# One decoder layer on one core: a load moved forward in the queue, a late wait, sums in halves, key rows by ScalarE, one activation moved

## The chip, the core and the metric

The kernel runs on one core of one Trainium2 chip. Its engines are TensorE (PE; PEld is its loading of weights), VectorE (DVE), ScalarE (ACT), GpSimd (POOL) and SyncE (SP, which here only issues DMAs); each has a queue of its own and they meet by semaphores. The metric is the device time of one execution in microseconds (us).

## The reference, cut to what matters

```
x = x + mamba(layernorm(x))                 # x: 8 batches x 224 rows x 512
x = x + cross_attention(layernorm(x), ctx)  # 16 heads of 32; ctx: 8 x 750 x 256
x = x + moe(layernorm(x))                   # 4 experts, the 2 likeliest for each row

mamba:  h[d, n] = h[d, n] * exp(A[d, n] * dt[d]) + dt[d] * x[d] * B[n]   # 224 steps in order
        y[d] = sum over the 16 n of h[d, n] * C[n];  y = (y + x * D) * silu(z);  return y @ W_out
attention: softmax((q Wq + bq)(k Wk + bk)^T / sqrt(32)) (v Wv + bv), then @ Wo + bo
moe:    p = softmax(gelu(x @ rW1 + rb1) @ rW2 + rb2)
        for each of its 2 experts: out += p * (gelu(x @ We1 + be1) @ We2 + be2)
```

## The kernel before, in words

Four stages follow one another, each in a block of its own; a block ends when all its engines and the DMAs that it awaits are done. They are the input products of the Mamba part, the state space (`state_space`, about 335 to 1017 us of the span), the attention with the router (`attention`, 1017 to 1826 us) and the experts (`experts`, from 1826 us).

**State space.** The work is 64 units (8 batches x 8 blocks of 128 channels), each in 4 segments of 56 time steps. For each segment TensorE fills PSUM, VectorE runs the scan (L917) and GpSimd multiplies the states by C (L804, counted by `hc_done`); the 16 states are then added up by TensorE, as products of the identity with `hc` into `yps`. For all units but the last this is `sums` (L955): for each state one product over all 224 columns, its four segments at once. The last unit's is `last_sums` (L959 to L968): it goes segment by segment, awaits each by `hc_done`, and has 4 x 16 products of 56 columns. Each float32 product shows as two records in the trace. `outputs` (DVE, L899 and L904) then makes `y`, and SP stores it (L705).

**Attention.** Every engine walks the same list `steps()` (iteration `it` from -1 to 9, slot `sl` from 0 to 15), and its order is written out by hand. With a = it + 1, c = it - 1 and last = it - 2, iteration `it` does the scores and softmax of batch `it` (one head a slot), the first half of batch a (Mamba's output product `project` L1699, the residual `residual1` L1305, the norm L1322 to L1339, `turn_norm` L1712, the queries L1726), the output and hidden layer of batch c, and the routing of batch `last`. In a slot, TensorE makes scores for two halves of the rows (L1633), VectorE takes their negated maxima (L1299, into `nmax`), ScalarE turns two such rows into the queries (L1549), TensorE makes the turned scores (L1659) with the key rows, ScalarE exponentiates (L1543), GpSimd adds up key tiles (`row_sum`, L1255 to L1261), and TensorE multiplies by the values (`values`, L1672) and by ones (`row_sums`, L1683).

`k3` holds the keys in its first 96 partitions; the two more rows (96 and 97) hold 1 and 0 in turn, by head parity, for all of its eight head places. They are written once: GpSimd sets them to zero (L1224) and adds a one-hot column (L1227 to L1229), which SP loads (L1178). Then GpSimd sets constants, waits for the residual of batch 0 and adds the output bias to it (`with_bias`, L1271, slot 13 of iteration -1). ScalarE first waits for three small loads (`w_loaded`) and scales Wq and bq (L1586).

SP's queue in iteration -1: `load_g(1)` at slot 5; stores of the first queries and `load_first_queries` at slot 8 (12 loads, L1164); `load_values` at slot 10 (4 loads of 375 KB, L1142); seven weights and constants at slot 11 (Wo, rb1, rW1, rW2, rb2, two small ones: L1219); `load_x(1)` at slot 14 (L1129, 448 KB: batch 1's rows of x into `xt`, after waits for `x1b_done` and `xn_done`). In iteration 0 follow `load_g(2)` at slot 5 (L1124, 896 KB) and `load_keys(2)` at slot 6 (L1135, three loads of 375 KB). `residual1(1, 0)`, in DVE's queue at slot 2 of iteration 0 between the two maxima, awaits `x_loaded`.

`gelu(last)` (ScalarE, L1572) stands in slot 0, behind that slot's exponentials and ahead of `turned_max`. In iteration 8 (`it == B`) only three heads' exponentials are left, in slots 0 to 2. The product of the gelu, `logit_parts` (L1762), stands in slot 4 of TensorE's queue, behind the values of slot 3.

**Experts.** Tiles of 256 rows go through 16 hidden blocks. VectorE makes the low parts of the hidden values (`results`, L2080) and at the end of a tile adds the second bias `b2` (L2086). `first` of expert 0 makes low parts of weights (L2055), the gates (L2059 to L2061) and then waits for `b2_loaded`, ahead of all tiles; SP issues that load at L1944.

## Time and profile before

| | |
|---|---|
| three runs | 2675.36, 2679.37, 2680.34 us; median 2679.37 |
| the profiled execution, its own time | 2675.31 us |
| its span | 2673.5 us |
| PE / PEld / DVE / ACT / POOL busy | 2404.6 / 1976.3 / 1452.0 / 1219.3 / 1373.0 us |
| mean granted TensorE clock | 0.948 of full |

All times in rows are us from the start of the span unless marked ns. A timeline row gives start, duration, engine, line, operation and operands; a time in square brackets is the idle time of that engine before it and what ended it. A row with xN merges N instructions that follow one another, from the first's start to the last's end. SPq is SP's queue issuing DMAs. A granted clock of 1.00 is TensorE's 2.4 GHz, 0.50 is 1.2 GHz.

### The profile page before, as it was taken

Reading aid. Unit: us, or ns where it says so; the run is one execution under the profiler, and the core shown is the slowest. Engines: PE = TensorE matmul, PEld = TensorE weight load, DVE = VectorE, ACT = ScalarE, POOL = GpSimd, SP = SyncE. Lnnn points to the kernel's source line nnn. Section 1 sums busy time; section 2 is a strip of 40 time slices with the busy share of each in tenths; the row PEclk is TensorE's granted clock in tenths of the full one; section 3 lists DMA queues with packets and bytes.
Section 4 is the critical chain, followed back from the end, with each engine's and each line's share of the span. In section 5 each row is a group of like instructions: output and inputs, shape, how many; then the busy total and the mean of one; then the engine's idle time right before and its main releaser. Section 6 shows DMA issues by size and latency. Waiting matters only on the chain. (4 is left out here: it accounts for less than half of the span.)

```text
span 2673.5 us, 39214 instructions
## 1 busy us (share of the span) xinstructions
PE 2404.6 (90%) x14240; PEld 1976.3 (74%) x14240; DVE 1452.0 (54%) x2034; ACT 1219.3 (46%) x2645; POOL 1373.0 (51%) x947
## 2 busy tenths in 40 slices
PE   7999499999999997589999999884989989998994
PEld 6867388888888885457766667564878878888883
DVE  7714599999999982355766666644121121121222
ACT  4345377777777651334544444433323333333331
POOL 2323477777777773365556656635460450019712
PEclk9999699999999998689999999886989999999997
DMA  4326956666666563455554655605230130003413
GB/s 121 125 69 220 268 177 208 195 188 174 200 199 207 165 188 101 129 116 122 136 135 115 143 120 124 156 21 170 79 112 22 63 118 16 16 31 95 116 34 118
DMA packets 235990, 341.72 MB, mean 128 GB/s; under 512 B 34706, under 2 KB 164306, under 8 KB 234690
## 3 DMA queue, kind: packets, MB, share of 16 engines
q1 hardware_dynamic: 213250, 279.89, 37.6%
q0 software_dynamic: 13728, 47.19, 5.7%
q10 hardware_dynamic: 8864, 12.72, 1.4%
q8 instruction: 86, 1.41, 0.2%
q14 instruction: 62, 0.51, 0.1%
HBM read 212.08 MB, written 127.65 MB: 127 GB/s over the span
## 5 line engine op out<-in xcount | busy, mean ns | idle before, releaser
L917 DVE TENSOR_TENSOR_SCAN s_h<-s_decay,s_ub 128x928 f32<-128x928 f32 x256 | 527.3, 2080 | 13.9 <-PE s_ub L944 7.1
L955 PE MATMUL s_yps<-s_hc,identity 128*128 128x224 f32 x2016 | 423.1, 353 | 0.0
L2080 DVE TENSOR_TENSOR e_hl<-e_ps,e_hh 128x256 fp32r<-128x256 f32 x256 | 108.6, 425 | 571.6 <-ACT e_ps L2130 571.2
L847 ACT ACTIVATE s_decay<-s_dt,s_A 128x224 f32<-128x224 f32 x1024 | 387.9, 470 | 20.8 <-DVE s_h L917 18.8
L955 PEld LDWEIGHTS s_yps<-s_hc,identity 128*128 128x128 f32 x2016 | 362.5, 190 | 0.8 <-issue 0.5
L1299 DVE TENSOR_REDUCE t_nmax<-t_ps 112x1 fp32r<-112x752 f32 x256 | 240.3, 938 | 218.8 <-PE t_ps L1633 218.0
L1255 POOL TENSOR_TENSOR t_part<-t_pT 125x672 f32<-125x672 f32 x128 | 206.9, 1616 | 275.1 <-ACT t_pT L1543 271.7
L2129 ACT ACTIVATE e_hh<-e_ps,e_b 128x256 fp32r<-128x256 f32 x256 | 122.0, 477 | 432.7 <-PE e_ps L2156 432.4
L2154 PE MATMUL e_ps<-e_xTh,e_w1h 128*128 128x256 f32 x1024 | 292.9, 286 | 23.3 <-DVE e_xTl L2072 23.3
L1543 ACT ACTIVATE t_pT<-t_ps 125x448 f32<-125x448 f32 x384 | 181.2, 546 | 273.7 <-PE t_ps L1659 266.9
L804 POOL TENSOR_TENSOR s_hc<-s_h,s_Cc 128x896 f32<-128x896 f32 x128 | 247.5, 1939 | 90.2 <-DVE s_h L917 47.4
L804 POOL TENSOR_TENSOR s_hc<-s_h,carry 128x896 f32<-128x896 f32 x128 | 247.6, 1940 | 88.9 <-DVE s_h L917 47.6
L2155 PE MATMUL e_ps<-e_xTl,e_w1h 128*128 128x256 f32 x1024 | 291.8, 285 | 0.0
L2156 PE MATMUL e_ps<-e_xTh,e_w1l 128*128 128x256 f32 x1024 | 290.9, 284 | 0.0
L1980 POOL TENSOR_TENSOR e_w1h<-carry,e_one 128x2048 fp32r<-128x2048 f32 x13 | 46.9, 3608 | 376.4 <-PE e_ps L2156 376.2
L1633 PE MATMUL t_ps<-t_k,t_q 96*112 96x376 f32 x512 | 187.7, 449 | 49.1 <-DVE t_nmax L1299 44.8
L2154 PE MATMUL e_ps<-e_w2h,e_hh 128*128 128x512 f32 x512 | 206.0, 402 | 22.1 <-DVE e_hl L2080 22.1
L2154 PEld LDWEIGHTS e_ps<-e_xTh,e_w1h 128*128 128x128 f32 x1024 | 197.6, 193 | 34.4 <-issue 24.6
L2155 PEld LDWEIGHTS e_ps<-e_xTl,e_w1h 128*128 128x128 f32 x1024 | 197.3, 193 | 9.3
L2156 PE MATMUL e_ps<-e_w2h,e_hl 128*128 128x512 f32 x512 | 202.7, 396 | 0.0
L2155 PE MATMUL e_ps<-e_w2l,e_hh 128*128 128x512 f32 x512 | 202.2, 395 | 0.0
L2156 PEld LDWEIGHTS e_ps<-e_xTh,e_w1l 128*128 128x128 f32 x1024 | 198.7, 194 | 0.0
(231 smaller groups left out, 4607.3 us busy)
## 6 DMA issues: line engine op xcount, KB each, us to landing
s_ut<-ut_d SPq DMA_DIRECT2D x192, 128.0 KB, 3.3
carry<-in_L_ffn_We POOLq DMA_DIRECT2D x24, 1024.0 KB, 5.7
t_k<-kh_d SPq DMA_DIRECT2D x64, 375.0 KB, 6.3
xs_d<-s_zero SPq DMA_DIRECT2D x30, 512.0 KB, 3.6
ut_d<-a_x SPq DMA_DIRECT2D x32, 448.0 KB, 5.4
kh_d<-s_kh SPq DMA_DIRECT2D x32, 375.0 KB, 2.8
kl_d<-s_kl SPq DMA_DIRECT2D x32, 375.0 KB, 3.1
v_d<-s_v SPq DMA_DIRECT2D x48, 250.0 KB
```

Of the source, the lines that this page charges most:

```text
L804: nc.gpsimd.tensor_tensor(hc[:, u % 2, k], h[:, u % 2, k, :, 2:SLOT], Cc[b % 2][:, k], ALU.mult).then_inc(hc_done, 1)
L847: ins = nc.scalar.activation(decay[:, u % 2, :, n, 2:SLOT], dts[:, u % 2].rearrange("p (s t) -> p s t", s=NSEG), ACT.Exp, scale=A[:, u % C ...
L917: nc.vector.tensor_tensor_scan(h[:, u % 2, k].rearrange("p n t -> p (n t)"), decay[:, u % 2, k].rearrange("p n t -> p (n t)"), ub[:, s % 2 ...
L955: ins = nc.tensor.matmul(yps[:, u % 2, 0:L], ident[:], hc[:, u % 2, :, n], start=(n == 0), stop=(n == NS - 1))
L1255: nc.gpsimd.tensor_tensor(part[:], p[:, 0:3], p[:, 3:6], ALU.add).then_inc(sum_step, 1)
L1299: nc.vector.tensor_reduce(nmax[:, u, h:h + 1], ps[0:TT, 0:2, 0:EVEN], AX.XY, ALU.max, negate=True).then_inc(max_done, 1)
L1543: nc.scalar.activation(pT[:, g % PT, 2 * i:2 * i + 2], ps[0:CT, TURN_BANK + i, 0:2 * L].rearrange("p (i t) -> p i t", i=2), ACT.Exp).then_ ...
L1633: ins = nc.tensor.matmul(ps[0:TT, i, 0:EVEN], q3[0:ROWS3, b % 2, h, u * TT:(u + 1) * TT], k3[0:ROWS3, J % 2, h % 4, i * (CTX - EVEN):i * ( ...
L2129: nc.scalar.activation(hh[:, c % RING], hidden_in, ACT.Gelu, bias=bias).then_inc(S["h_high"], 1)
L2154: nc.tensor.matmul(out, sh, mh, start=first, stop=False)
L2155: nc.tensor.matmul(out, sh, ml, start=False, stop=False)
L2156: return nc.tensor.matmul(out, sl, mh, start=False, stop=last)
```

## The change

The edits of the diff:

- `last_sums` goes by halves: it waits for segments 0 and 1, makes 16 products of 112 columns, waits for segments 2 and 3 and makes 16 more.
- The two extra key rows are written by ScalarE in four activations (scale 0 and a bias column of the identity), ahead of its wait for the small loads. GpSimd's memset and four additions, the one-hot tile and its load go, and so does its first semaphore.
- `load_x(1)` moves from slot 14 to slot 9 of iteration -1 in SP's queue; the later batches' loads stay at slot 14.
- In iteration 8 the gelu moves from slot 0 to slot 4.
- The wait for `b2_loaded` moves from behind the gates to the bias addition at each tile's end.
- The wait for `y_done` in `last_sums` stands ahead of the first wait for `hc_done`.

```
--- before.py
+++ after.py
@@ -958,13 +958,12 @@
 
             def last_sums(u):
 
-                for k in range(NSEG):
-                    pe.wait_ge(hc_done, NSEG * u + k + 1)
-                    if k == 0:
-                        pe.wait_ge(y_done, u - 1)
+                pe.wait_ge(y_done, u - 1)
+                for half in range(2):
+                    pe.wait_ge(hc_done, NSEG * u + 2 * half + 2)
                     for n in range(NS):
-                        ins = nc.tensor.matmul(yps[:, u % 2, k * SEG:(k + 1) * SEG], ident[:], hc[:, u % 2, k, n],
-                                               start=(n == 0), stop=(n == NS - 1))
+                        ins = nc.tensor.matmul(yps[:, u % 2, half * L // 2:(half + 1) * L // 2], ident[:],
+                                               hc[:, u % 2, 2 * half:2 * half + 2, n], start=(n == 0), stop=(n == NS - 1))
                 ins.then_inc(sum_done, 1)
 
             def keys_values(u, pieces):
@@ -1045,7 +1044,6 @@
         wo, rw1, rw2 = sb("wo", [P, KC, DM]), sb("rw1", [P, KC, RH]), sb("rw2", [P, RC, DK])
         bqc, bvc, rb1c = sb("bqc", [P, KC]), sb("bvc", [P, KC]), sb("rb1c", [P, RC])
         bor, rb2r = sb("bor", [P, DM]), sb("rb2r", [P, E])
-        onehot = sb("onehot", [ROWS3 + 2, 2])
         ones = sb("ones", [CT, DK])
         xb = sb("xb", [TT, 2, 2, DM])
         k3 = sb("k3", [ROWS3 + 2, 2, 4, CTX], F32R)
@@ -1082,7 +1080,7 @@
         x2_stored = sem("x2_stored")
         route, shifted, exped, masked, ranked, rank_read, indexed, counted = (
             sem(n) for n in ("route", "shifted", "exped", "masked", "ranked", "rank_read", "indexed", "counted"))
-        consts_set, rows_zeroed, rows_set, q_scaled = (sem(n) for n in ("consts_set", "rows_zeroed", "rows_set", "q_scaled"))
+        consts_set, rows_set, q_scaled = (sem(n) for n in ("consts_set", "rows_set", "q_scaled"))
         score_mm, max_done, turn_mm, turn_done = (sem(n) for n in ("score_mm", "max_done", "turn_mm", "turn_done"))
         st_mm, exp_done, sum_step, sum_done = (sem(n) for n in ("st_mm", "exp_done", "sum_step", "sum_done"))
         pv_mm, sums_mm, rinv_done, o_read, o_done = (sem(n) for n in ("pv_mm", "sums_mm", "rinv_done", "o_read", "o_done"))
@@ -1092,7 +1090,7 @@
         q_mm, q_high, q_low = sem("q_mm"), sem("q_high"), sem("q_low")
         rh_mm, rh_pre, rh_done, lp_mm, lp_done, lg_mm, lg_done = (
             sem(n) for n in ("rh_mm", "rh_pre", "rh_done", "lp_mm", "lp_done", "lg_mm", "lg_done"))
-        N_W, N_REST, N_SET = 3, 7, 22
+        N_W, N_REST, N_SET = 2, 7, 22
         ROUTE = 18
         FAR = float(E * SLOTS)
 
@@ -1175,7 +1173,6 @@
                     We1[0].rearrange("(k p) n -> p k n", p=P)[:, :, g * DM:(g + 1) * DM]
                 sp.dma_start(carry[:, n * KC * DM:(n + 1) * KC * DM].rearrange("p (k n) -> p k n", n=DM), src).then_inc(w_first[n], 16)
 
-            sp.dma_start(onehot[ROWS3:ROWS3 + 2], ident_in[0:2, 0:2]).then_inc(w_loaded, 16)
             for dst, src in ((bqc[:], bq), (bvc[:], bv)):
                 sp.dma_start(dst, src).then_inc(w_loaded, 16)
             load_keys(0)
@@ -1205,10 +1202,12 @@
                     sp.dma_start(x2_d[c], xb[:, c % 2]).then_inc(x2_stored, 16)
                 if it == -1 and sl == 5:
                     load_g(1)
+                if it == -1 and sl == 9:
+                    load_x(1)
                 if it == -1 and sl == 10:
                     for j in range(KC):
                         load_values(j)
-                if sl == 14 and among(a + 1, B):
+                if sl == 14 and it >= 0 and among(a + 1, B):
                     load_x(a + 1)
                 if it == B - 1 and 1 <= sl <= 4:
                     load_first_weights(sl - 1)
@@ -1221,13 +1220,6 @@
 
         @block.gpsimd
         def _(pool):
-            nc.gpsimd.memset(k3[ROWS3:ROWS3 + 2].bitcast(F32), 0.0).then_inc(rows_zeroed, 1)
-            pool.wait_ge(rows_zeroed, 1)
-            pool.wait_ge(w_loaded, 16 * N_W)
-            for r in range(4):
-                nc.gpsimd.tensor_scalar(k3[ROWS3:ROWS3 + 2, :, r], k3[ROWS3:ROWS3 + 2, :, r].bitcast(F32),
-                                        onehot[ROWS3:ROWS3 + 2, r % 2:r % 2 + 1], None, ALU.add).then_inc(rows_set, 1)
-            pool.wait_ge(rows_set, 4)
             nc.gpsimd.memset(ones[:], 1.0).then_inc(consts_set, 1)
 
             for t in state_sems:
@@ -1581,6 +1573,11 @@
                 act.wait_ge(shifted, b + 1)
                 nc.scalar.activation(p[:], p[:], ACT.Exp).then_inc(exped, 1)
 
+
+            two = slice(ROWS3, ROWS3 + 2)
+            for r in range(4):
+                nc.scalar.activation(k3[two, :, r], ident[two, 0:2].unsqueeze(2).to_broadcast([2, 2, CTX]), ACT.Identity, scale=0.0,
+                                     bias=ident[two, ROWS3 + r % 2:ROWS3 + r % 2 + 1]).then_inc(rows_set, 1)
             act.wait_ge(w_loaded, 16 * N_W)
             for t in (wq, bqc[:]):
                 nc.scalar.activation(t, t, ACT.Copy, scale=float(DK) ** -0.5).then_inc(q_scaled, 1)
@@ -1596,7 +1593,7 @@
                     high_queries(a, 2 * sl - 16)
                 if among(s - LAG, STEPS):
                     exponentials(s - LAG)
-                if sl == 0 and among(last, B):
+                if sl == (4 if it == B else 0) and among(last, B):
                     gelu(last)
                 if sl == 7 and among(a, B):
                     turned_norm(a, 0, 0)
@@ -2082,6 +2079,7 @@
                     wait(dve, "l2_mm", n * HC + HC)
 
                     wait(dve, "y_stored", n * 16)
+                    wait(dve, "b2_loaded", 16)
                     for s in range(HALVES):
                         v.tensor_tensor(y[:, s], ps[:, Y_BANK + s], b2[:, e], ALU.add).then_inc(S["y_done"], 1)
 
@@ -2091,7 +2089,6 @@
                         for n in range(2, 4):
                             low_weights(n)
                         gates()
-                        wait(dve, "b2_loaded", 16)
 
                 expert_tiles(dve, e, first, results)
```

## Rows read from the trace of the kernel before
**Rows 1.** Windows: us; busy (count) of PE, PEld, DVE, ACT, POOL; clock; DMA.
```profile
1000.00:1017.20 17.20, 14.04 (x126) 13.90 (x125) 1.61 (x4) 0.00 (x0) 0.78 (x1) 1.00 0.07 25
...
1066.00:1090.30 24.30, 2.00 (x8) 0.66 (x6) 1.60 (x3) 1.81 (x2) 0.00 (x0) 0.62 0.66 194
```
**Rows 2.** Timeline, end of the state space: start us, us, engine, line.
```profile
998.85 1.93 POOL L804 TENSOR_TENSOR s_hc<-s_h,s_Cc 128x896 f32<-128x896 f32 x1 [1.12 <-DVE s_h L917]
...
996.61 3.19 PE L955 MATMUL s_yps<-s_hc,identity 128*128 128x224 f32 x16
999.64 14.39 PE L966 MATMUL s_yps<-s_hc,identity 128*128 128x56 f32 x128
```
**Rows 3.** Timeline, the attention's first 25 us.
```profile
1019.64 1.91 ACT L1586 ACTIVATE carry<-carry 128x2048 f32<-128x2048 f32 x1 [22.23 <-DMA t_bvc<-in_L_xattn_bv]
...
1022.44 16.57 POOL L1228 TENSOR_SCALAR t_k<-t_k,t_onehot 2x1500 fp32r<-2x1500 f32 x4
...
1032.97 0.69 DVE L1305 TENSOR_TENSOR carry<-t_ps,carry 112x512 f32<-112x512 f32 x1 [5.44 <-PE t_ps L1699]
...
1034.64 0.23 DVE L1322 TENSOR_SCALAR t_rstd<-t_mv 112x2 f32<-112x2 f32 x1
...
1036.68 3.05 DVE L1339 TENSOR_SCALAR t_xn<-carry,t_mv,t_rstd 112x512 f32<-112x512 f32 x2
```
**Rows 4.** Timeline near 1146 us, then line L1339 over the span (ns min/median/max).
```profile
1146.00 2.49 POOL L1271 TENSOR_TENSOR t_xb<-carry,t_bor 112x512 f32<-112x512 f32 x2
...
1146.34 2.29 DVE L1456 TENSOR_SCALAR t_oT<-t_rinv,t_bvc 128x224 f32<-128x224 f32 x1
...
L1339 DVE TENSOR_SCALAR t_xn<-carry,t_mv,t_rstd x16: 529/547/2604, 1036.7 to 1627.2; 112x512 f32<-112x512 f32 x16
```
**Rows 5.** Timeline, 1058 to 1093 us.
```profile
1058.96 10.86 SPq L1142 DMA_DIRECT2D t_v<-v_d  x4
...
1061.84 1.88 PE L1699 MATMUL t_ps<-carry 128*112 128x512 f32 x4
...
1064.11 0.94 DVE L1299 TENSOR_REDUCE t_nmax<-t_ps 112x1 fp32r<-112x752 f32 x1 [1.12 <-PE t_ps L1633]
...
1083.62 0.33 SPq L1129 DMA_DIRECT2D carry<-in_x  x1
1088.70 0.69 DVE L1305 TENSOR_TENSOR carry<-t_ps,carry 112x512 f32<-112x512 f32 x1 [23.65 <-DMA carry<-in_x]
...
1092.29 3.62 PE L1699 MATMUL t_ps<-carry 128*112 128x512 f32 x4
```
**Rows 6.** Line L1129, the seven later loads of x rows: time to landing.
```profile
DMA to landing us min/median/max: 5.1/7.3/8.3
```
**Rows 7.** Line L1135, the 96 key loads, to landing; timeline, first scores of keys 2.
```profile
DMA to landing us min/median/max: 3.7/5.6/10.5
...
1118.19 0.60 PE L1633 MATMUL t_ps<-t_k,t_q 96*112 96x376 f32 x2
```
**Rows 8.** Timeline, end of the attention's last batch.
```profile
1759.23 1.70 ACT L1572 ACTIVATE t_rh<-t_rh 128x1792 f32<-128x1792 f32 x1
...
1762.40 1.28 ACT L1543 ACT_TABLE_LOAD   x1 [0.92 <-PE t_ps L1659]
...
1765.19 1.61 POOL L1255 TENSOR_TENSOR t_part<-t_pT 125x672 f32<-125x672 f32 x1 [3.02 <-ACT t_pT L1543]
1766.75 4.71 PE L1672 MATMUL t_ps<-t_pT,t_v 125*32 125x224 f32 x48 [0.79 <-issue]
...
1772.53 0.59 PE L1683 MATMUL t_ps<-t_rsum,t_ones 125*32 125x224 f32 x8
```
**Rows 9.** The second-layer bias: issue, landing of line L1944, DVE behind its wait.
```profile
1841.33 0.51 SPq L1944 DMA_DIRECT2D e_b<-in_L_ffn_be  x1
...
DMA to landing us min/median/max: 9.0/9.0/9.0
...
1852.01 1.09 DVE L2080 TENSOR_TENSOR e_hl<-e_ps,e_hh 128x256 fp32r<-128x256 f32 x3 [0.41 <-DVE e_gate L2061]
```

More of the change, by code:

```diff
@@ L959, in last_sums @@
             def last_sums(u):
-                for k in range(NSEG):
-                    pe.wait_ge(hc_done, NSEG * u + k + 1)
-                    if k == 0:
-                        pe.wait_ge(y_done, u - 1)
+                pe.wait_ge(y_done, u - 1)
+                for half in range(2):
+                    pe.wait_ge(hc_done, NSEG * u + 2 * half + 2)
                     for n in range(NS):
-                        ins = nc.tensor.matmul(yps[:, u % 2, k * SEG:(k + 1) * SEG], ident[:], hc[:, u % 2, k, n],
-                                               start=(n == 0), stop=(n == NS - 1))
+                        ins = nc.tensor.matmul(yps[:, u % 2, half * L // 2:(half + 1) * L // 2], ident[:],
+                                               hc[:, u % 2, 2 * half:2 * half + 2, n], start=(n == 0), stop=(n == NS - 1))
                 ins.then_inc(sum_done, 1)
@@ L1047, in attention @@
         bor, rb2r = sb("bor", [P, DM]), sb("rb2r", [P, E])
-        onehot = sb("onehot", [ROWS3 + 2, 2])
         ones = sb("ones", [CT, DK])
@@ L1084, in attention @@
             sem(n) for n in ("route", "shifted", "exped", "masked", "ranked", "rank_read", "indexed", "counted"))
-        consts_set, rows_zeroed, rows_set, q_scaled = (sem(n) for n in ("consts_set", "rows_zeroed", "rows_set", "q_scaled"))
+        consts_set, rows_set, q_scaled = (sem(n) for n in ("consts_set", "rows_set", "q_scaled"))
         score_mm, max_done, turn_mm, turn_done = (sem(n) for n in ("score_mm", "max_done", "turn_mm", "turn_done"))
@@ L1094, in attention @@
             sem(n) for n in ("rh_mm", "rh_pre", "rh_done", "lp_mm", "lp_done", "lg_mm", "lg_done"))
-        N_W, N_REST, N_SET = 3, 7, 22
+        N_W, N_REST, N_SET = 2, 7, 22
         ROUTE = 18
@@ L1207, in _ @@
                     load_g(1)
+                if it == -1 and sl == 9:
+                    load_x(1)
                 if it == -1 and sl == 10:
@@ L1210, in _ @@
                         load_values(j)
-                if sl == 14 and among(a + 1, B):
+                if sl == 14 and it >= 0 and among(a + 1, B):
                     load_x(a + 1)
@@ L1223, in _ @@
         def _(pool):
-            nc.gpsimd.memset(k3[ROWS3:ROWS3 + 2].bitcast(F32), 0.0).then_inc(rows_zeroed, 1)
-            pool.wait_ge(rows_zeroed, 1)
-            pool.wait_ge(w_loaded, 16 * N_W)
-            for r in range(4):
-                nc.gpsimd.tensor_scalar(k3[ROWS3:ROWS3 + 2, :, r], k3[ROWS3:ROWS3 + 2, :, r].bitcast(F32),
-                                        onehot[ROWS3:ROWS3 + 2, r % 2:r % 2 + 1], None, ALU.add).then_inc(rows_set, 1)
-            pool.wait_ge(rows_set, 4)
             nc.gpsimd.memset(ones[:], 1.0).then_inc(consts_set, 1)
@@ L1582, in probabilities @@
                 nc.scalar.activation(p[:], p[:], ACT.Exp).then_inc(exped, 1)
+            two = slice(ROWS3, ROWS3 + 2)
+            for r in range(4):
+                nc.scalar.activation(k3[two, :, r], ident[two, 0:2].unsqueeze(2).to_broadcast([2, 2, CTX]), ACT.Identity, scale=0.0,
+                                     bias=ident[two, ROWS3 + r % 2:ROWS3 + r % 2 + 1]).then_inc(rows_set, 1)
             act.wait_ge(w_loaded, 16 * N_W)
@@ L1598, in _ @@
                     exponentials(s - LAG)
-                if sl == 0 and among(last, B):
+                if sl == (4 if it == B else 0) and among(last, B):
                     gelu(last)
@@ L2084, in results @@
                     wait(dve, "y_stored", n * 16)
+                    wait(dve, "b2_loaded", 16)
                     for s in range(HALVES):
@@ L2093, in first @@
                         gates()
-                        wait(dve, "b2_loaded", 16)
                 expert_tiles(dve, e, first, results)
```

1 line of the change is left out of this document (removed).

## The prediction

> **What bounds the kernel now.** I first read the page's busy shares: TensorE is busy most of the span, so a gain has to come from stretches in which it idles, works slowly or does work that can shrink. The windows show two. From 1000 to 1017.2 us TensorE works alone, at the full clock, and nobody else has work [rows 1]. From 1066 to 1090.3 us all four engines stand still together [rows 1]. The timeline says what ends each. The first is `last_sums`: 128 records of 56 columns, 14.39 us, begun when the last segment's product with C was already running (998.85 to 1000.78), so that from the second segment on it waits for nobody [rows 2]. The second is DVE's residual of batch 1, which sat 23.65 us for a DMA that SP issued only at 1083.62 us, behind the values and the weights; DVE holds the next maximum behind it, and everybody waits for that maximum [rows 5]. The same reading of the attention's first 25 us and of its end gives two short stalls on the chain [rows 3, 8].
>
> **The parts.** Sums are made against the profiled execution's own 2675.31 us.
>
> *Sums in halves.* 64 float32 products become 32, so 128 records become 64. A record costs 14.39 / 128 = 0.112 us at 56 columns and 3.19 / 16 = 0.199 us at 224 [rows 2]. At 112 columns the price lies between. If the 0.112 us is the loading of the 128 columns of weights, the same for both, then 64 x 0.112 = 7.2 us, a gain of 7.2; at the price of 224 columns it is 12.8 us, a gain of 1.6. Streaming twice 56 columns more cannot cost less than before, so 7.2 is the best. I take it: scaled down from 224 columns, the streaming of 112 takes 0.10 us, less than 0.112. Of the two waits the second is over at 1000.78, while the first half runs until 1003.2, so they cost nothing. Here a rule speaks against the change. The Trainium skill, page "TensorE: Matmul & The Clock Gate", section "Measured speedup vs the span model", says that a weight load overlaps a product in flight only when they use different row groups; here both use all rows. By that rule and the page's load price (columns / 1.2 ns, 107 ns) a record would be load plus streaming, 154 ns at 56 columns and 200 ns at 112, and the gain at measured start would be 14.4 - 12.8 = 1.6 us, for a sum of 30.1. The 0.112 us that the trace has at 56 columns is well under that 154, so trace and rule disagree. From the last sum to the block's end all follows in a row (DVE's two operations, the store), so the gain is whole.
>
> *Key rows by ScalarE.* Off GpSimd go 16.57 us and a memset. On ScalarE come four activations of 1500 elements a partition; from 1.91 us for 2048 [rows 3] each takes 1.40 us, 5.6 in all, from 1017.2 to 1022.8. Wq is then scaled by 1024.8 instead of 1021.5; even at the 4.1 us that GpSimd took for each it would be 1035.5, ahead of the end of the normalisation at 1039.7, which the first query needs too. Hidden, at no cost. The gain is elsewhere: DVE's normalisation took 3.05 us for two [rows 3] instead of 2 x 0.55 [rows 4], its first one ending just after GpSimd's last of the four at 1039.01; DVE waited for GpSimd. Gone alone, this gives 2.05 us. But what is next on GpSimd? It now reaches `with_bias` early, and runs its 2.49 us from 1033.7, when DVE's second residual of batch 0 (L1305) is done [rows 3], to 1036.2. In its middle, at 1034.64, DVE has the small operation L1322 [rows 3]. In rows 4 just such a DVE operation, begun beside GpSimd's pair, lasted 2.29 us, to the end of both. So L1322 ends at 1036.3, 1.4 us later than before, and of 2.05 us some 0.6 stay. The Trainium skill, page "SBUF — State Buffer", has the shared ports held for one whole instruction by whoever began first; by that rule L1322 would get them between GpSimd's two, at 1035.0, and the gain would be some 1.9 us, the sum 37.0. The row speaks for the pair as a whole. I take 0.6, between 0.6 and 2.05. The dropped one-hot load frees SP 0.3 us long before it matters.
>
> *Rows of batch 1.* Issued behind the first queries, at 1058.96 where the first value load now stands [rows 5]. Both waits in `load_x` are over by then. This load took 5.1 us to land (1083.62 to 1088.7), later batches' up to 8.3 [rows 6], so x is there between 1064.1 and 1067.3. DVE wants it after the maximum of 1064.11, at 1065.05 [rows 5]. So 23.65 us go, and 0 to 2.2 come back; I take 0, for only small loads stand ahead. What is moved past are four value loads and seven weight loads: they get later by the wire time of 448 KB, a microsecond or two. The values are wanted some 25 us after, the weights in iteration 1. What is late next: SP gets through the weights only by about 1084.5, as before, since these are held by the queue and not by engines. Then come the 896 KB of `load_g(2)` and the three key loads, the last issued near 1086. These land 3.7 to 10.5 us later [rows 7], at 1089.7 to 1096.5; TensorE wants them at 1118.19 - 23.65 = 1094.54 [rows 7]. That gives 0 to 2.0 us; with g in front I take 0.5. The stall also left TensorE cold: four records of `project` took 3.62 us behind it and 1.88 before it [rows 5], where the granted clock had been 1.2 and 2.4 GHz. This gives back 1.7 us in the first slot; as low stretches may come elsewhere, the bounds are -1.7 and +3.5. Together 23.65 - 0.5 + 1.7 = 24.9 us, between 17.7 and 27.2.
>
> *The gelu.* In iteration 8 it took ScalarE with a table load 3.0 us ahead of the turned maximum, and another table load of 1.28 us before the exponentials [rows 8]: 4.3 us off their chain. But the chain ends at GpSimd, whose sums release the product with ones at 1772.53; GpSimd had only 3.02 us of idle time before the last but one of them [rows 8], its scatter being just ahead. So 3.0 us. Behind the exponentials the gelu and its load (3.0 us) run beside the values, 4.71 us on TensorE [rows 8]; without that cover the 3.0 would come back. I take 3.0, between 0 and 3.0.
>
> *The bias.* Issued at 1841.33, landed 9.0 us later at 1850.3; DVE worked on the gates until 1851.6 and began the low parts at 1852.01 after 0.41 us [rows 9]. The wait was hidden by the gates: no gain beyond 0.4. It now stands in front of the bias additions of all 16 tiles, with the load long there. Queued behind it are only these and, for the store, ACT's DMA; on the chain stand the four tiles that end an expert, at most 4 x 0.41 = 1.6 us. I take 0.
>
> Sum: 7.2 + 0.6 + 24.9 + 3.0 = 35.7 us, so 2639.6 for this execution. The median of three runs is 4.06 us above it; carried over, 2643.7 us.
>
> **The rivals.** *A, the forecast*, all four gains within their bounds (31 to 40 us): 0.72.
> *B, the DMA queue gives part of it back.* x, the values, g(2) or keys(2) land so late that a new DMA wait of 5 to 12 us stands in slots 2 to 8. For: in 1066 to 1090 the queue was never empty, 0.66 busy [rows 1], and nothing makes these bytes fewer. Against: the key loads' slowest landing leaves 2 us. Price 8: 2651.7. Chance 0.12.
> *C, a record costs load and streaming*, as the skill's rule has it or as the row at 224 columns would: the gain on the sums is 1.6 instead of 7.2, 2649.3. The 56-column row speaks against it. 0.09.
> *D, the change does not do what it says*: x is not what DVE waited for, or its new place still waits, because `x1b_done` comes late. Then 10.8 us stay: 2668.6. Against: issue plus landing, 1083.62 + 5.1, is just the 1088.70 at which DVE went on. 0.05.
> *E, slower.* The keys of group 2, in slot 8 of iteration 0, behind x, values, weights and g: each microsecond beyond 1094.5 is one on the chain. It decides from 1094.5 + 35.7 = 1130 us, 44 us after the issue; the slowest of 96 took 10.5 [rows 7]. At 50 us it would give 2685. 0.02 with all else that could make it not faster.
>
> **The numbers.** A, C and most of B are inside 2634 to 2655: the low end is the best of each part (39.9 us) against the fastest run, 2635.5, a little widened; the high end is 25 us of gain against the median. What a measurement of this kernel can tell from no change is about 0.2%, 5.4 us. Faster by more: A to D, 0.98. Within it 0.01, slower 0.01.
>
> **What would show it.** `last_sums` as 64 records in about 7.2 us; DVE's L1322 lasting 1.6 us and its two normalisations 1.1; x issued before the values and no wait of 20 us at L1305; any key wait at the first scores of group 2 under 2 us; GpSimd without idle time before its last two sums and the product of the gelu right behind the values; no change around L2080. I am wrong if the sums take over 9 us, if a DMA wait over 5 us stands between slots 2 and 9, or if the stage from 1118 us on is not the same length as before.

## The result and the profile after

| us | before | after |
|---|---|---|
| median (range, runs) | 2679.86 (2675.36 to 2681.37, 4) | 2647.03 (2643.26 to 2648.53, 4) |
| the profiled execution, its own time | 2675.31 | 2648.53 |
| its span | 2673.5 | 2646.7 |
| PE / DVE / ACT / POOL busy | 2404.6 / 1452.0 / 1219.3 / 1373.0 | 2391.3 / 1459.1 / 1224.4 / 1351.7 |
| mean granted TensorE clock | 0.948 | 0.955 |

The ratio is 0.9878, 95% interval [0.9861, 0.9895]: 32.8 us less by the medians, 26.8 by the two profiled executions. The two differ because the profiled execution of before is as fast as the fastest of its four (2675.36), and that of after is the slowest of its own; the rows below come from these two. The forecast was 2643.7, within 2634 to 2655. So the total is right within 3.3 us. The parts are less so. I cut both timelines at the same instructions (first product of the attention's block, first transpose, first maximum of slots 0, 3, 7 and 8 and of batch 1, last maximum, last product with ones, first product of the experts); each number is a difference of start times in the trace.

| stretch, us | before | after | difference |
|---|---|---|---|
| up to the attention's block | 1017.3 | 1012.1 | -5.2 |
| block to first transpose | 22.06 | 20.27 | -1.8 |
| to the first maximum | 14.85 | 13.75 | -1.1 |
| to slot 3 | 37.11 | 12.53 | -24.6 |
| slots 3 to 7 | 20.25 | 16.23 | -4.0 |
| slot 7 to slot 8 | 7.28 | 13.13 | **+5.85** |
| to batch 1 | 42.87 | 42.06 | -0.8 |
| batch 1 to the last maximum | 591.91 | 599.71 | **+7.8** |
| to the last product with ones | 18.92 | 15.96 | -3.0 |
| to the experts' first product | 62.93 | 63.45 | +0.5 |
| to the end | 838.04 | 837.49 | -0.55 |

They add up to the span's 26.8 us. Three rows are positive: +5.85, which I had sized at 0.5, +7.8, which I had not seen at all, and +0.5 at the end of the attention, which the gelu gives back. The -1.1 between the first transpose and the first maximum I didn't forecast, and no run isolates it.

The start of the changed stretch, from the timeline of after (start, duration, engine, line, operation); it answers to [rows 2, 3]:
```profile
1001.58 7.29 PE L965 MATMUL s_yps<-s_hc,identity 128*128 128x112 f32 x64
...
1012.10 5.83 ACT L1579 ACTIVATE t_k<-identity 2x1500 fp32r<-2x1500 f32 x4 [12.75 <-PEq L597]
...
1028.66 2.51 POOL L1263 TENSOR_TENSOR t_xb<-carry,t_bor 112x512 f32<-112x512 f32 x2 [11.49 <-DVE carry L1297]
...
1029.49 0.49 DVE L1314 TENSOR_SCALAR t_rstd<-t_mv 112x2 f32<-112x2 f32 x1
...
1031.79 1.00 DVE L1331 TENSOR_SCALAR t_xn<-carry,t_mv,t_rstd 112x512 f32<-112x512 f32 x2
```
The last sums are 64 records in 7.29 us, 0.114 each, where 128 took 14.39: 7.1 less. They began 1.9 us later in the span than before, after 1000 us of unchanged code; in the kernels below that share the new sums the block's start lies anywhere from 1008.2 to 1014.1, so those 1.9 us are not the change's. The small operation L1314 lasted 0.49 us, not the 1.6 that I forecast, and ended at 1029.98, just behind the end of GpSimd's first addition (1029.95).

Rows and keys in iteration 0, same timeline, against [rows 5, 7]:
```profile
1049.94 0.37 SPq L1127 DMA_DIRECT2D carry<-in_x  x1
1050.35 11.36 SPq L1140 DMA_DIRECT2D t_v<-v_d  x4
...
1055.24 0.68 DVE L1297 TENSOR_TENSOR carry<-t_ps,carry 112x512 f32<-112x512 f32 x1
...
1074.40 2.05 SPq L1133 DMA_DIRECT2D t_k<-kh_d  x1
1076.49 1.13 SPq L1133 DMA_DIRECT2D t_k<-kl_d  x1
1077.67 0.46 SPq L1133 DMA_DIRECT2D t_k<-kh_d  x1
...
1078.55 3.38 PE L1669 MATMUL t_ps<-t_pT,t_v 125*32 125x224 f32 x48
...
1087.15 0.84 PE L1630 MATMUL t_ps<-t_k,t_q 96*112 96x376 f32 x2 [5.22 <-issue]
...
1088.03 0.94 DVE L1291 TENSOR_REDUCE t_nmax<-t_ps 112x1 fp32r<-112x752 f32 x1 [9.51 <-PE t_ps L1630]
```
The residual has no wait left. But before the first scores of key group 2 TensorE sat 5.22 us, though nothing on the engines was late. "Issue" here means only that the profile found no releaser. The windows around it (us; busy and count of PE, PEld, DVE, ACT, POOL; clock; DMA share and GB/s), first those that answer to [rows 1]:
```profile
1000.00:1012.10 12.10, 8.88 (x74) 8.71 (x73) 2.41 (x5) 0.00 (x0) 1.94 (x2) 1.00 0.20 59
1066.00:1070.00 4.00, 2.58 (x15) 1.82 (x14) 2.97 (x4) 2.70 (x4) 3.07 (x4) 1.00 1.01 327
1070.00:1074.00 4.00, 2.67 (x12) 1.65 (x11) 3.52 (x9) 2.92 (x6) 1.55 (x3) 0.52 1.03 408
1074.00:1078.00 4.00, 3.90 (x16) 3.18 (x17) 1.66 (x3) 2.47 (x5) 3.66 (x4) 0.50 1.08 295
1078.00:1082.00 4.00, 3.93 (x52) 2.00 (x50) 0.52 (x1) 0.54 (x1) 2.30 (x3) 0.70 1.10 176
1082.00:1087.00 5.00, 0.00 (x0) 0.00 (x0) 0.00 (x0) 0.00 (x0) 0.00 (x0) 1.00 0.68 161
```
From 1082 to 1087 all engines stood still together while the DMA engines, full since 1066, were at 0.68. It is the picture of [rows 1] again, five microseconds instead of twenty.

The end of the attention, against [rows 8]:
```profile
1738.29 1.28 ACT L1564 ACT_TABLE_LOAD   x1
1738.37 4.54 PE L1669 MATMUL t_ps<-t_pT,t_v 125*32 125x224 f32 x48 [0.79 <-issue]
1738.40 1.62 POOL L1247 TENSOR_TENSOR t_part<-t_pT 125x672 f32<-125x672 f32 x1
...
1742.73 0.95 PE L1759 MATMUL t_ps<-t_rh,t_rw 128*32 128x224 f32 x16
...
1745.76 0.77 PE L1680 MATMUL t_ps<-t_rsum,t_ones 125*32 125x224 f32 x8 [2.09 <-POOL t_rsum L1253]
...
1749.01 9.02 PE L1736 MATMUL t_ps<-t_wo,t_oT 128*112 128x512 f32 x16 [1.64 <-DVE t_oT L1448]
```
GpSimd's 3.02 us of idle time is gone, and the gelu runs beside the values. It now ends at 1741.29, so its product has it in time.

Where the +7.8 us came from shows in slot 13 of batch 1 in this timeline:
```profile
1200.54 2.55 POOL L1263 TENSOR_TENSOR t_xb<-carry,t_bor 112x512 f32<-112x512 f32 x2 [1.05 <-issue]
...
1201.08 3.70 DVE L1448 TENSOR_SCALAR t_oT<-t_rinv,t_bvc 128x224 f32<-128x224 f32 x1
...
1203.04 1.60 POOL L1247 TENSOR_TENSOR t_part<-t_pT 125x672 f32<-125x672 f32 x1
```
A DVE operation of 0.34 us, begun beside GpSimd's bias additions, lasted 3.70 us: to the end of both and of GpSimd's next one as well. The next maximum stands behind it.

### The profile page after: what moved, and what is told of

The parts are those of the page before. It is cut to its first block and busy times, and to the rows that moved or that the text cites. A ratio compares the mean times of both kernels' runs of the same rounds, so it can differ in the third digit from the quotient of the medians.

```text
span 2646.7 us, 39098 instructions
## 1 busy us (share of the span) xinstructions
PE 2391.3 (90%) x14176; PEld 1967.2 (74%) x14176; DVE 1459.1 (55%) x2034; ACT 1224.4 (46%) x2649; POOL 1351.7 (51%) x942
## 5 line engine op out<-in xcount | busy, mean ns | idle before, releaser
L2077 DVE TENSOR_TENSOR e_hl<-e_ps,e_hh 128x256 fp32r<-128x256 f32 x256 | 108.5, 425 | 571.1 <-ACT e_ps L2127 570.7
```

## The experiments

The change is a bundle, so first its parts. All ratios are against the kernel before, run beside it.

| kernel | median (range, runs), us | ratio, 95% |
|---|---|---|
| e1_x_late | 2667.16 (2652.61 to 2675.94, 10) | 0.9964 [0.9944, 0.9984] |
| e2_weights_late | 2652.28 (2640.38 to 2660.03, 5) | 0.9916 [0.9884, 0.9948] |
| e3_x_only | 2656.31 (2653.10 to 2662.84, 4) | 0.9930 [0.9903, 0.9957] |
| e5_bias_later | 2639.00 (2636.18 to 2642.24, 4) | 0.9860 [0.9838, 0.9882] |
| f1_rows_gpsimd | 2640.66 (2639.54 to 2644.29, 4) | 0.9876 [0.9860, 0.9893] |
| f2_gelu_early | 2642.40 (2638.30 to 2643.54, 4) | 0.9877 [0.9860, 0.9893] |
| f3_b2_early | 2636.65 (2631.19 to 2640.72, 4) | 0.9855 [0.9837, 0.9874] |
| f4_rw1_late | 2630.25 (2626.98 to 2634.25, 4) | 0.9830 [0.9813, 0.9846] |
| g0_changed_again | 2644.72 (2640.05 to 2656.99, 6) | 0.9889 [0.9869, 0.9908] |
| e6_bias_later_before | 2668.21 (2663.05 to 2672.64, 10) | 0.9973 [0.9959, 0.9988] |
| f5_sums_whole | 2637.91 (2633.09 to 2641.84, 4) | 0.9876 [0.9855, 0.9896] |
| g1_best | 2631.35 (2625.60 to 2634.67, 4) | 0.9840 [0.9817, 0.9863] |

The kernel before had medians of 2674.45, 2674.89 and 2675.35 us beside them (first four rows, next four, last four). Medians of different groups of four rows are best compared by their ratios.

**The rows of x: one undone, one alone.** e1 is the changed kernel with the load back in slot 14:
```
-                if it == -1 and sl == 9:
-                    load_x(1)
-                if sl == 14 and it >= 0 and among(a + 1, B):
+                if sl == 14 and among(a + 1, B):
                     load_x(a + 1)
```


> The changed kernel with batch 1's rows of x back at slot 14 of iteration -1, behind values and weights. Theory (the stall was the place of this load in SP's queue; the forecast's 23.65 us, 0.9 more by the fourth slot, 4.0 from TensorE's full clock until slot 7, less a wait of 5.2 us for the keys of group 2): a DMA stall of 22 to 25 us returns at the residual of batch 1, the key wait is gone, first maximum to first of batch 1 is 105 to 109 us instead of 84.0, the time is 22 to 25 us above the changed kernel's. Rival (other edits of the change took most of the stall away, such as GpSimd reaching its bias addition early): the stall is under 10 us and the time within 10 us of the changed kernel's.

The stall came back. Timeline of e1, DVE's residual of batch 1:
```profile
1077.39 0.69 DVE L1295 TENSOR_TENSOR carry<-t_ps,carry 112x512 f32<-112x512 f32 x1 [21.94 <-DMA carry<-in_x]
```
By the same cuts as above e1 has 33.72 us to slot 3 (+21.2), 19.68 for slots 3 to 7 (+3.45) and 7.53 from slot 7 to 8 (-5.6). So the wait for keys is the price of having removed the wait for x, and the slots behind the stall had been slow with it, not only the first: the granted clock over slots 3 to 7 is 0.67 before, 0.76 in e1 and 0.85 in the changed kernel. From the first maximum of slot 0 to that of batch 1 e1 takes 103.8 us, just under the 105 to 109 expected. From the first maximum to slot 8 that is 60.93 us against 41.89 of the changed kernel, a net 19.0; the medians of e1 and g0 lie 22.4 apart, their ratios 0.0075 or 20.1.

e3 is the kernel before with only this move:
```
+                if it == -1 and sl == 9:
+                    load_x(1)
-                if sl == 14 and among(a + 1, B):
+                if sl == 14 and it >= 0 and among(a + 1, B):
```


> The kernel before with only the load of batch 1's x moved to slot 9. Theory (the move alone is worth its stall, plus clock, less the key wait): 20 to 25 us less than before, first maximum to first of batch 1 at 84 to 86 us. If the move needs GpSimd freed of the key rows: its bias addition of batch 0 ends at 1046.7, before SP reaches slot 9 at 1058.9, so no difference is expected; the rival says SP waits for it and less than 15 us are gained.

18.1 us by the medians, with 14.68 us from slot 7 to 8, and 64.64 - 45.10 = 19.5 from the first maximum to slot 8. The changed kernel's own trace has 64.64 - 41.89 = 22.75 there. The part is worth 18 to 23 us, below my 24.9 and for e3 below the 20 to 25 expected of it (87.1 us to batch 1 instead of 84 to 86); rival B would have left 16.9. The truth lay between the two.

**What holds the keys up.** e2 moves all seven weight loads of slot 11 from iteration -1 to iteration 0:
```
-                if it == -1 and sl == 11:
+                if it == 0 and sl == 11:
                     sp.wait_ge(consts_set, 2)
```


> The changed kernel with the seven weight and constant loads of iteration -1 (3 MB) moved behind the queries of iteration 0 in SP's queue (slot 11). Theory (the 5.2 us in which TensorE waits before slot 8 are the key loads of group 2 queued behind g(2), weights and values): these keys land 5 us or more before they are wanted, the wait is gone, slot 7 to slot 8 takes 7 to 8 us instead of 13.1, and the time is 4 to 6 us lower if no later DMA takes its place. Rival (the wait is the values' or the engines' own order, not the queue): slot 7 to slot 8 stays at 12 to 13.5 us, no time gained. A third way: the weights now delay x, values or keys in slots 12 to 15, and the gain is given back there.

Slot 7 to 8 fell from 13.13 to 7.78 us, so the weights in front were indeed what delayed the keys. They did it in two ways. In the changed kernel the last of the three keys was issued 31.5 us after the first maximum of slot 0, in e2 25.6 us after it; and from issue to landing the three took, in the changed kernel, in e2 and in f4 (below), in this order:
```profile
DMA to landing us min/median/max: 8.7/9.1/9.4
...
DMA to landing us min/median/max: 4.2/5.7/7.0
...
DMA to landing us min/median/max: 6.7/8.1/11.5
```
So the last key was there 40.9 us after that maximum in the changed kernel and 32.6 in e2, and TensorE was ready for it at 35.8 and 35.9. But batch 0's remainder grew from 42.06 to 47.17. Timeline of e2, first scores of batch 1, whose keys were issued from 1114.64 us on:
```profile
1127.68 0.94 PE L1630 MATMUL t_ps<-t_k,t_q 96*112 96x376 f32 x2 [5.26 <-DMA t_k<-kh_d]
```
Here the profile names the releaser: the key load. The weights now stood in front of the next group of keys, and the wait went there nearly whole (5.35 us off, 5.1 on); the median is no lower than the changed kernel's. f4 moves only the largest, rW1 (2 MB), and puts it right behind the keys of group 2 (on top of e5, below):
```
-                    for dst, src in ((wo[:], rows(Wo)), (rb1c[:], rb1), (rw1[:], rows(rW1)), (rw2[:, :, 0:E], rows(rW2)),
+                    for dst, src in ((wo[:], rows(Wo)), (rb1c[:], rb1), (rw2[:, :, 0:E], rows(rW2)),
...
+                if it == 0 and sl == 7:
+                    sp.dma_start(rw1[:], rows(rW1)).then_inc(rest_loaded, 16)
```


> The changed kernel with the later bias addition, and with one weight load (rW1, 2 MB of the 3) moved behind the key loads of group 2 in SP's queue (slot 7 of iteration 0). Theory (these keys wait for 3 MB of weights in the queue; moving all of them to slot 11 only carried the wait to the next batch's first slot): slot 7 to slot 8 takes 7.5 to 9 us instead of 12 to 13, and slot 8 to the first of batch 1 stays at 42 to 43 us: 3 to 5 us faster. Rival (any place gives it back: values and queries' stores of slots 8 and 9 stand behind it now): slot 8 to batch 1 grows by what slot 7 gains.

Timeline of f4, keys, rW1 and the first scores of group 2:
```profile
1069.23 0.32 SPq L1133 DMA_DIRECT2D t_k<-kh_d  x1
1069.60 0.43 SPq L1133 DMA_DIRECT2D t_k<-kl_d  x1
1070.07 0.43 SPq L1133 DMA_DIRECT2D t_k<-kh_d  x1
1070.55 0.43 SPq L1196 DMA_DIRECT2D t_rw<-in_L_ffn_rW  x1
...
1081.69 0.57 PE L1632 MATMUL t_ps<-t_k,t_q 96*112 96x376 f32 x2 [1.10 <-issue]
```
TensorE waits 1.10 us instead of 5.22; slot 7 to 8 takes 9.00 us, and nothing took its place: the rest of batch 0 is 42.24 and the middle batches 590.65. The last key's landing did not get shorter (11.5 us); it was issued 6.0 us earlier. The median is the lowest of its four rows, 6.4 us under f3's and 10.4 under f1's, the two others of the four that keep the gelu late; their intervals touch at 0.9837 to 0.9846 for f3 and are apart for f1.

**The middle batches.** e5 is the changed kernel with GpSimd's bias additions one slot later, except for batch 0; e6 has the same edit on the kernel before:
```
-                if sl == 13 and among(it + 1, B):
+                if sl == (13 if it == -1 else 14) and among(it + 1, B):
                     with_bias(it + 1)
```


> The changed kernel with GpSimd's addition of the output bias one slot later (14 instead of 13) for all batches but the first. Theory (in slot 13 of the later batches this 2.5 us pair runs into DVE's scaling of the attention's output, which waits until GpSimd is through, and how often it does is a matter of phase: the seven slot-13 gaps of the changed kernel sum to 44.5 us against 34.5 before): all slot-13 gaps at 4.3 to 4.6 us, first of batch 1 to the last maximum at 585 to 590 us instead of 599.7, the time 8 to 13 us below the changed kernel's. Rival (the longer gaps are a DMA's or the clock's): gaps of 6 to 9 us stay in several batches and the time stays within 3 us.

Line L1448 over the whole span, shortest, median and longest in ns, first in the changed kernel:
```profile
L1448 DVE TENSOR_SCALAR t_oT<-t_rinv,t_bvc x32: 335/337/3696, 1099.7 to 1748.6; 128x224 f32<-128x224 f32 x32
```
then in e5:
```profile
L1448 DVE TENSOR_SCALAR t_oT<-t_rinv,t_bvc x32: 335/336/1619, 1101.4 to 1739.2; 128x224 f32<-128x224 f32 x32
```
In e5 the same two operations no longer meet in slot 13; its timeline has the DVE one first:
```profile
1203.16 0.34 DVE L1448 TENSOR_SCALAR t_oT<-t_rinv,t_bvc 128x224 f32<-128x224 f32 x1
...
1206.71 2.54 POOL L1263 TENSOR_TENSOR t_xb<-carry,t_bor 112x512 f32<-112x512 f32 x2
```
The time from the first maximum of slot 13 to that of slot 14, batches 1 to 7, is 7.5, 6.6, 9.2, 6.1, 4.6, 6.1, 4.4 us in the changed kernel and 4.4 in all seven in e5, 13.8 us less; the stretch from batch 1 to the last maximum goes from 599.71 to 588.39. So the collisions carry the +7.8: slot 13 alone is 10.1 us longer than before. Was that the change's doing?

> The kernel before with GpSimd's bias addition of all batches but the first one slot later. Theory (the same collisions cost the kernel before 4 us in its profiled execution and more in its slower ones): all slot-13 gaps at 4.3 to 4.7 us, 3 to 8 us less than before. Rival (only the changed kernel's phase meets them): within 2 us of before.

> The changed kernel once more, unaltered, on the chip of this call. Theory (slot 13 of the later batches is a matter of phase from execution to execution): the seven slot-13 gaps sum to another value than the 44.5 us of its first trace, somewhere between 33 and 48, while block start to the first transpose (20.3), the fourth slot (12.5 from the first maximum) and slot 7 to 8 (12 to 13.5) repeat within 1 us; the time is 26 to 35 us below the kernel before. Rival (the gaps belong to the changed kernel's order): the same batches have the same gaps within 0.5 us.

In the kernel before the gaps of slot 13 were 4.4 but for one of 8.0, and 590.63 us in e6 stand beside 591.91: 1.3 us in the trace, though the median fell by 7.1 (interval 0.9959 to 0.9988). g0, the changed kernel once more, has 608.57 us there with gaps of up to 9.3. So both kernels can collide. Whether GpSimd and DVE meet is a matter of how the engines stand to each other: before, GpSimd's pair began at 1233.53, after DVE's operation at 1232.72, in the slot in which they overlapped after. The two traces of the changed kernel have collisions in most batches and the one of before in one; whether the change makes them more frequent, or one trace of before was a lucky one, these runs don't settle. The unprofiled executions speak for luck: g0's profiled one is the slowest of its six, and by the medians moving the additions takes 7.1 us off the kernel before, and off the changed kernel 4.8 (ratio 0.9878 to 0.9860) to 7.8 (0.9889 to 0.9860), which is no more.

What a meeting costs depends on when it begins. All fourteen traces together have 37 in which DVE's operation (L1314, L1448 and their likes in the other kernels) began while GpSimd was in the first of its two bias additions, of 1.3 us each. DVE's operation ended 0.02 to 0.18 us behind the end of the second in the 14 begun 0 to 0.48 us after GpSimd's first, behind a third instruction in the 5 begun 0.51 to 0.60 us after it, behind the first alone in the 17 begun 0.64 to 0.99 us after it, and behind the third in one begun at 1.22. So a shift of a tenth of a microsecond can cost three. Why it falls out so, no run shows. The trace of before, too, has one that ended behind the first addition, in slot 13 of batch 5:
```profile
1488.05 2.54 POOL L1271 TENSOR_TENSOR t_xb<-carry,t_bor 112x512 f32<-112x512 f32 x2 [1.27 <-issue]
...
1488.77 0.68 DVE L1456 TENSOR_SCALAR t_oT<-t_rinv,t_bvc 128x224 f32<-128x224 f32 x1
```

**The small parts**, each undone on top of e5, so that the collisions don't blur them. f1, key rows by GpSimd again (its memset, four additions, the one-hot tile and load):
```
+            for r in range(4):
+                nc.gpsimd.tensor_scalar(k3[ROWS3:ROWS3 + 2, :, r], k3[ROWS3:ROWS3 + 2, :, r].bitcast(F32),
+                                        onehot[ROWS3:ROWS3 + 2, r % 2:r % 2 + 1], None, ALU.add).then_inc(rows_set, 1)
...
-            for r in range(4):
-                nc.scalar.activation(k3[two, :, r], ident[two, 0:2].unsqueeze(2).to_broadcast([2, 2, CTX]), ACT.Identity, scale=0.0,
-                                     bias=ident[two, ROWS3 + r % 2:ROWS3 + r % 2 + 1]).then_inc(rows_set, 1)
```


> The changed kernel with the later bias addition (GpSimd's slot 14), and with the two extra key rows written by GpSimd again, with the one-hot load. Theory (DVE's normalisation waits for GpSimd's running instruction, and with the rows gone DVE's small operation L1314 is let in between GpSimd's two bias additions): block start to the first transpose back from 20.3 to 22.1 us or up to 24.2 (it depends on where in GpSimd's 4.07 us instruction DVE comes), DVE's two normalisations back at 3 us or more, the rest as before: 2 to 4 us slower than with the rows on ScalarE. Rival (the forecast's 0.6 us, the gain comes from elsewhere, such as ScalarE's start): the stretch stays within 0.7 us of 20.3.

Timeline of f1, the block's start:
```profile
1013.38 16.57 POOL L1229 TENSOR_SCALAR t_k<-t_k,t_onehot 2x1500 fp32r<-2x1500 f32 x4
1025.58 0.23 DVE L1323 TENSOR_SCALAR t_rstd<-t_mv 112x2 f32<-112x2 f32 x1
...
1027.63 3.05 DVE L1340 TENSOR_SCALAR t_xn<-carry,t_mv,t_rstd 112x512 f32<-112x512 f32 x2
```
These are the durations of [rows 3] again, and the first transpose comes 22.07 us into the block. In the ten kernels with rows by ScalarE it comes after 19.90 to 21.64. Most of that spread lies ahead of the second residual, in TensorE's 15 products: 15.7 us from the block's start at a granted clock of 0.89, 16.7 to 17.1 us at 0.82 to 0.84 in f2, f5 and g0. From the second residual to the first transpose it takes 6.4 us in before, e6 and f1 and 4.6 in nine of the ten, so the part is worth 1.8 us; the medians (2640.66 against 2639.00 of e5 and 2636.65 of f3) can't resolve it. With the rows on GpSimd it can also be worse: in e3 DVE's small operation began at 1034.03, 0.13 us after one of GpSimd's four, and lasted 3.97 us; the first transpose came after 24.18 us.

g1 takes that further (f4, the sums of f5, and GpSimd's first bias additions held until DVE's normalisation is done):
```
                 if b == 0:
                     pool.wait_ge(bo_loaded, 16)
+                    pool.wait_ge(xn_done[0], 2)
```


> Put together: the changed kernel with the later bias addition, rW1 behind the key loads of group 2, sums as a whole, and the first batch's bias addition held until its two normalisations are done. Theory: slot 13 at 4.4 us, slot 7 to 8 at 9 us, block start to the first transpose at 19.9 to 20.1 us (DVE's L1314 at 0.17 to 0.23 us instead of 0.49), 9 to 13 us less than the changed kernel of this call. Rival: GpSimd's held addition makes the load of batch 1's x late (then a stall at its residual), or the key wait is taken over by another DMA.

Timeline of g1:
```profile
1028.03 0.17 DVE L1315 TENSOR_SCALAR t_rstd<-t_mv 112x2 f32<-112x2 f32 x1
...
1031.15 2.51 POOL L1264 TENSOR_TENSOR t_xb<-carry,t_bor 112x512 f32<-112x512 f32 x2 [15.40 <-DVE t_xn L1332]
```
Alone, L1315 takes 0.17 us. So beside GpSimd it had lost 0.3 us (0.49), and 4.25 us from the second residual to the first transpose against 4.57 is that 0.3. As a whole g1 is no faster than f4.

f2, the gelu in slot 0 again in iteration 8:
```
-                if sl == (4 if it == B else 0) and among(last, B):
+                if sl == 0 and among(last, B):
```


> The changed kernel with the later bias addition, and with the gelu of iteration 8 back in slot 0. Theory (GpSimd's sums are the chain's end there, and had 3.0 us of idle time to lose): last maximum to the last product with ones 18.9 us instead of 15.9, 3 us slower. Rival (it is the product of the gelu behind the values that counts): within 1 us.

Timeline of f2, end of the attention's last batch:
```profile
1731.41 1.61 POOL L1247 TENSOR_TENSOR t_part<-t_pT 125x672 f32<-125x672 f32 x1 [3.01 <-ACT t_pT L1535]
...
1741.83 8.61 PE L1736 MATMUL t_ps<-t_wo,t_oT 128*112 128x512 f32 x16 [2.00 <-DVE t_oT L1448]
```
GpSimd's idle 3.01 us is back, and 18.92 us from the last maximum to the product with ones. The next stretch tells something else: up to the experts it takes 62.75 us here and 64.92 in f3. The 16 output products L1736 took 8.61 us in f2, 9.02 in the changed kernel and 10.02 in f3. Windows of exactly these products, in f2:
```profile
1741.80:1750.50 8.70, 8.61 (x16) 3.32 (x16) 1.14 (x5) 1.49 (x2) 0.00 (x0) 0.82 0.06 21
```
and in f3:
```profile
1737.30:1747.40 10.10, 10.02 (x16) 3.73 (x16) 1.15 (x5) 1.49 (x2) 0.00 (x0) 0.71 0.05 18
```
The granted clock was 0.82 of full in the one and 0.71 in the other. Both stretches together are 81.67 to 81.85 us in the four traces with the gelu early and 79.20 to 80.98 in the ten with it late. So of the 3.0 us between 0.7 and 2.7 stay. The medians (2642.40 against 2639.00 of e5 and 2636.65 of f3) point the same way; the intervals of f2 and e5 overlap.

f3, the wait for `b2` behind the gates again:
```
-                    wait(dve, "b2_loaded", 16)
                     for s in range(HALVES):
...
                         gates()
+                        wait(dve, "b2_loaded", 16)
```


> The changed kernel with the later bias addition, and with the wait for the second bias back behind the gates. Theory (the load lands ahead of the gates' end, so the wait is worth nothing wherever it stands): the first low part of a hidden block begins at the same distance behind the gates (0.4 us idle), the experts' stage within 0.5 us, the time within 2 us. Rival (16 waits more at the tiles' ends cost something): up to 1.6 us faster than with them.

DVE's first L2077 had 0.41 us of idle time before it in f3, as in [rows 9] and in the changed kernel. The medians of f3 and e5 overlap. The wait cost nothing in either place.

f5, the last sums in one piece, 16 products of 224 columns behind one wait:
```
+                pe.wait_ge(hc_done, NSEG * (u + 1))
+                for n in range(NS):
+                    ins = nc.tensor.matmul(yps[:, u % 2, 0:L], ident[:], hc[:, u % 2, :, n], start=(n == 0), stop=(n == NS - 1))
```


> The changed kernel with the later bias addition, and with the last unit's sums as 16 products of 224 columns, awaited as a whole. Theory (at 112 columns a record costs the loading of its weights, 0.112 us as at 56; at 224 its streaming, 0.19): 32 records in 6.1 to 6.4 us, but begun 1.1 to 1.3 us later, behind the last product with C: within 0.5 us of the halves' 7.29 us. Rival (load and streaming of a record add up, as the skill's rule has it): 32 records would take 9 us or more, and the whole would be 3 us slower than the halves.

Timeline of f5:
```profile
997.32 1.93 POOL L804 TENSOR_TENSOR s_hc<-s_h,s_Cc 128x896 f32<-128x896 f32 x1 [1.12 <-DVE s_h L917]
...
999.40 6.29 PE L964 MATMUL s_yps<-s_hc,identity 128*128 128x224 f32 x32 [1.14 <-DVE s_y L904]
1005.80 0.46 DVE L899 SCALAR_TENSOR_TENSOR s_yps<-s_late,s_D,s_yps 128x224 f32<-128x224 f32 x1 [6.48 <-PE s_yps L964]
```
The products are a microsecond shorter, 6.29 us for 32 (0.197 each), but wait for the last segment. From GpSimd's last product to DVE's next operation it takes 8.48 us here, 8.18 with halves (1000.80 to 1008.98) and 15.29 before (998.85 to 1014.14). Halves are the better cut, by 0.3 us. No run takes the halves back alone, but this stretch repeats within 0.02 us wherever the code is the same: 15.3 in before, e3 and e6, 8.2 in the nine traces with halves.

The experiments also point to a kernel faster than both: f4, the changed kernel with rW1 behind the keys and the bias additions a slot later, 2630.25 us, 1.7% under the kernel before.

## Why the prediction was right, and where it was not

**Right in the sum for partly wrong reasons.** Forecast 35.7 us, measured 26.8 by the profiled executions and 32.8 by the medians. The misses went both ways, and that they left the medians only 3.3 us from the forecast is in part luck.

- *Sums in halves*: 7.2 forecast, 7.1 measured. A record has a price that the columns don't move between 56 and 112 (0.112 and 0.114 us), and at 224 one that they set (0.197). That the fixed price is the loading of weights is argued, from PEld's 13.90 us beside PE's 14.04 in [rows 1]. Rival C wanted 12.8 us for the 64 records. The rule of the Trainium skill's "TensorE: Matmul & The Clock Gate", which stands in the section "The mechanism" and not where the prediction put it, wanted as much; the trace has 7.29 and disagrees. The same section also names a load into the background weight buffer as one that overlaps, which the prediction left out.
- *Key rows by ScalarE*: 0.6 forecast, 1.8 measured. Hidden on ScalarE as said (5.83 us against 5.6). The step that failed is "the row speaks for the pair as a whole": L1314 ended in 0.49 us, just behind GpSimd's first addition, as the rule in the Trainium skill's "SBUF — State Buffer", section "Who interferes with whom", has it (the one who began first holds the ports for one whole instruction). By that rule I had 1.9. But in slot 13 DVE sat out two instructions ([rows 4]) or three (3.70 us above), which the rule doesn't give. [rows 4] is one meeting, begun 0.34 us after GpSimd; L1314 was to begin 0.94 us after it by my own numbers, and the trace of before had a meeting begun 0.72 us after, at 1488.77, that lasted 0.68 us.
- *Rows of batch 1*: 24.9 forecast; 22.75 in the changed kernel's trace, 18 to 20 by e1 and e3. The stall went whole. The term "with g in front I take 0.5" for the keys, bounds 0 to 2.0, was mis-sized: 5.22 us. Of its two halves the queue's was right: counted from the first maximum of slot 0, I had the last key issued at 31.8 us and landing 3.7 to 10.5 us later, and it was issued at 31.5 and landed 9.4 us later. The want was wrong: I had kept its old distance, 40.3 us, and TensorE was there at 35.8. It came early because the clock gave back more than I had allowed, and ahead of these keys: +1.7 for one slot, where slots 0 to 3 gave 0.9 and slots 3 to 7 another 4.0 (3.45 in e1); and even the 1.7 I had not taken off the want. At the old distance the same landing would have cost 0.6 us; so what the clock gave, the keys took. The landings were near the slow end of their range, 8.7 to 9.4 us for all three, with the DMA engines at 1.0 of their time from 1066 to 1082. e2 and f4 show the queue's side: with the weights, or rW1 alone, behind the keys, slot 7 to 8 takes 7.78 and 9.00 us instead of 13.13. In the kernel before, the 20 us of stall drained the same queue.
- *The gelu*: 3.0 forecast and 2.96 measured where I looked. Some of it was given back behind my last row, where TensorE's clock was lower: 0.5 in the changed kernel, up to 2.2 in others.
- *The bias*: nothing, as forecast.
- *The middle*: I was to be wrong if "the stage from 1118 us on is not the same length as before", and it wasn't: 7.8 us longer, 16.7 in g0. I had read the collision in [rows 4] and used it only for the block's start; that it decides slot 13 of every batch, by tenths of a microsecond of phase, I did not ask.

Of the rivals, B was the mechanism that came true (a new DMA wait over 5 us between slots 2 and 9, one of my signs of being wrong), at 5 us and not 8. In the eight traces with x early and all the weights in front of the keys this wait is 3.4 to 5.8 us, over 5 in three of them. With the collisions taken out on both sides (e5 and e6, ratios 0.9860 and 0.9973) the change is worth about 30 us, 5 to 6 less than the 35.7 forecast. The keys (4.7 more than forecast) and what the gelu gave back (0.5 to 2.2) are of that size; what the clock gave over my 1.7 and the 1.2 of the key rows went the other way, and a part of the account stays open.

## What to carry to other kernels

When you remove a stall, ask what the queue was doing in it: bytes that it drained unseen will be late next, and the large load that nobody wants yet belongs behind the small one that is wanted first. Price a load in a full queue at the slow end of its landing times, and take the time at which it is wanted from the timeline as the change will leave it: a removed stall can bring the want forward by more than its own length. And when a trace shows two engines colliding once, look for every place where their instructions could meet, since a few tenths of a microsecond of shift decide it.

## What was not expected of the hardware

- A float32 product with 128 columns of weights takes 0.112 us a record at 56 columns, 0.114 at 112 and 0.197 at 224, at a granted clock of 1.00.
- A DVE operation of 0.34 us that meets GpSimd's additions lasted 0.68, 2.29 [rows 4] or 3.70 us; one of 0.17 us lasted 0.49. It ended just behind one of GpSimd's instructions: the second when begun up to 0.48 us after GpSimd's first addition, the third at 0.51 to 0.60, the first at 0.64 to 0.99 (36 meetings; one at 1.22 ended behind the third).
- The same 16 output products at the attention's end took 8.61 us at a granted clock of 0.82 and 10.02 at 0.71, a mix of the two levels, in kernels that differ here in where the gelu stands. They took 8.5 to 8.6 us (0.82 to 0.83) in the four traces with the gelu early and 8.9 to 10.1 us (0.70 to 0.80) in the ten with it late; why these ten differ among themselves no run shows.
